# Two expert layers in groups of four and pairs of two, with twelve row fetches ahead and scatters and fetches by turns

## What is computed

```python
# first block, expert capacity 308
probs = softmax(x @ Wr + br); gates, ids = top_k(probs, 2)
h   = silu(einsum('ecd,edh->ech', xg, W1) + b1[:, None, :])     # xg: rows gathered by expert
out = einsum('ech,ehd->ecd', h, W2) + b2[:, None, :]
y   = zeros((N, D)).at[disp_tok].add(out * disp_g)              # scattered back by token

# second block
top_w, top_i = top_k(softmax(xf @ router_w.T), 2); top_w /= sum(top_w)
h = gelu(einsum('nc,ech->enh', xf, w1), approximate=False)
y = einsum('ne,enc->nc', comb, einsum('enh,ehc->enc', h, w2))
```

## Time and profile before

| | |
|---|---|
| time, median of three runs | 1128.98 us (1125.56 to 1130.19) |
| the profiled execution's own span | 1166.7 us |
| PE busy in it | 1021.1 us, 88% |
| DVE, ACT, POOL busy | 846.9, 796.1, 291.8 us |
| expert layer 0, first fetch to last scatter landed | 202.10 to 333.63 us |
| expert layer 1, likewise | 1034.77 to 1150.61 us |
| POOL's indirect DMAs, fetch and block scatter, median of one | 0.968 and 0.985 us |

### The profile page before, as it was taken

One profiled execution on the slowest core, in us unless ns is written; L12 is line 12 of the kernel. 1 busy time (PEld: TensorE's weight loads), 2 busy tenths in 40 slices (PEclk: granted clock), 3 DMA queues, 4 the chain that ended last, 5 costly groups with the idle time before them and its releaser, 6 DMA issues.

```text
span 1166.7 us, 22431 instructions
## 1 busy us (share of the span) xinstructions
PE 1021.1 (88%) x8264; PEld 490.1 (42%) x8268; DVE 846.9 (73%) x1585; ACT 796.1 (68%) x1174; POOL 291.8 (25%) x296
## 2 busy tenths in 40 slices
PE   9747667777888789999999999999999999977785
PEld 6412224777864322332223223232223332447785
DVE  3599997255334789999999999999999991361123
ACT  3653432445555569999999999999999999332122
POOL 0079871555325410000000000000000000036652
PEclk9969998898899889999999999999999999989898
DMA  3055533644123420011100111001111000066333
GB/s 106 1 188 185 194 108 110 199 123 121 55 89 117 143 72 19 17 35 34 35 22 15 35 35 35 19 18 35 35 34 20 17 4 5 3 193 204 116 94 124
DMA packets 57975, 87.94 MB, mean 75 GB/s; under 512 B 26240, under 2 KB 28664, under 8 KB 57484
## 3 DMA queue, kind: packets, MB, share of 16 engines
q1 hardware_dynamic: 51694, 75.52, 21.0%
q0 software_dynamic: 4544, 9.32, 2.6%
q10 hardware_dynamic: 1630, 1.67, 0.5%
HBM read 73.10 MB, written 12.94 MB: 74 GB/s over the span
## 4 chain that ended last, share of the span: by engine, by line
PE 68%; DVE 10%; issue 9%; DMA 4%; ACT 3%; another core or an unknown queue 2%; POOL 2%; SPq 1%; ACTq 0%; DVEq 0%; POOLq 0%
PE psum L959 24%; PE psum L945 22%; PE psum L1084 6%; PE psum L1070 6%; PE psum L949 2%; DVE ssm_h L1738 2%; PE psum L1053 1%; PE psum L789 1%; DVE tile_max L2018 1%; DMA w1r<-y_dram 1%; POOL h0T L1457 1%; DVE ssm_g L1747 1%; PE psum L769 1%; DVE proj_o L2014 1%
## 5 line engine op out<-in xcount | busy, mean ns | idle before, releaser
L1320 ACT ACTIVATE probs<-psum 128x1024 f32<-128x1024 f32 x512 | 505.5, 1041 | 15.1 <-PE psum L949 4.1
L2018 DVE TENSOR_REDUCE tile_max<-psum 128x1 f32<-128x512 f32 x720 | 456.3, 684 | 27.9 <-PE psum L945 26.4
L959 PE MATMUL psum<-probs,v_head 128*32 128x256 f32 (+1 forms) x3840 | 320.8, 406 | 0.7 <-ACT probs L1320 0.4
L945 PE MATMUL psum<-k_stack,q_stack 62*128 62x512 bf16 x994 | 311.2, 397 | 10.9 <-DMA q_stack<-q_dram 7.4
L949 PE MATMUL psum<-q_stack,k_stack 64*128 64x512 bf16 x1024 | 302.8, 384 | 4.1 <-DMA q_stack<-max_parts 3.7
L945 PEld LDWEIGHTS psum<-k_stack,q_stack 62*128 62x128 bf16 x994 | 92.1, 110 | 245.6 <-DVE tile_max L2018 116.5
L1509 POOL TENSOR_TENSOR max_parts<-row_max,no_shift 128x8 bf16<-128x8 f32 x32 | 6.4, 199 | 537.9 <-DVE row_max L1994 537.9
L959 PEld LDWEIGHTS psum<-probs,v_head 128*32 128x32 f32 x3840 | 75.7, 108 | 154.6 <-issue 102.9
L1084 PE MATMUL psum<-w_held,hid 128*128 (+1 forms) x624 | 92.6, 296 | 25.2 <-ACT hid L1379 11.2
L1070 PE MATMUL psum<-x_cols,w1r 128*128 128x128 f32 (+1 forms) x624 | 92.2, 296 | 10.3 <-issue 7.7
L1084 PEld LDWEIGHTS psum<-w_held,hid 128*128 128x128 f32 x624 | 83.7, 208 | 28.4 <-issue 27.2
(11 more groups left out here) (284 smaller groups left out, 1074.8 us busy)
## 6 DMA issues: line engine op xcount, KB each, us to landing
w1r<-w SPq DMA_DIRECT2D x78, 256.0 KB
ssm_b<-bc_dram SPq DMA_DIRECT2D x32, 512.0 KB, 4.1
k_stack<-k_dram SPq DMA_DIRECT2D x60, 120.0 KB
w_held<-w SPq DMA_DIRECT2D x16, 256.0 KB, 4.4
w1r<-y_dram SPq DMA_DIRECT2D x16, 256.0 KB, 5.2
q_stack<-q_dram SPq DMA_DIRECT2D x30, 96.0 KB
bc_p<-bc_dram SPq DMA_DIRECT2D x5, 512.0 KB, 5.7
xtok_dram<-x_tok SPq DMA_DIRECT2D x8, 256.0 KB, 2.4
```

Source lines behind the costliest of these rows:

```text
L945: mm(bank, queries, k_stack[rows, u, keys:keys + C], start=True, stop=True).then_inc(s1_ps, 1)
L959: i = mm(psum[32 * j:32 * j + VM, 7, lo:hi], v_head[:, u, kt, :], probs[:, kt % 4, j * C + lo:j * C + hi], start=kt == 0, stop=kt == KT - ...
L1320: f(probs[:, kt % 4, hf * HALF:(hf + 1) * HALF], banks(2 * slot, 2), ACT.Exp, scale=SCALE).then_inc(p_ready, 1)
L2018: v.tensor_reduce(top, bank, AX.X, ALU.max).then_inc(s1_read, 1)
```

## The change

Both expert layers are regrouped, and POOL's order is new:

- Fetches go straight into `x_cols`, which holds all 32 blocks; `x_got` and its ring are gone. One semaphore counts the fetches of each turn.
- Turns are made in groups (`TURNS`): blocks 0-1, 2-3, then seven groups of four. A group goes into one PSUM bank, and one instruction scales it into `x_cols`, in place.
- `up` and `down` go by pairs of items (20 "units", the last of one item), with four PSUM banks for `up` and four pairs of `hid`. Gelu takes a pair in one instruction; silu keeps four for each item.
- `rows` go by sets of four items (10 sets) in one copy, into buffers for all 39 items (in the space of `lane_hot`, in `y_sum`, and in a new tile); the ring of 6 is gone, and `put` is one semaphore.
- POOL issues 12 fetches, then for each block its scatter and the fetch of the block 12 further on. A scatter waits for its row set's copy.
- PE's order: turns 0 to 2 and units 0 and 1 up first; then for each unit u the turn that starts three units on (if one does), up(u+2), down(u). The gate spreads stand around the downs of units 1 and 2, the capacity rounds behind units 3 to 10, and `gates_turned` behind the loop.

```diff
+UNITS = [(i, min(i + 2, ITEMS)) for i in range(0, ITEMS, 2)]
+TURNS = [(0, 2), (2, 4)] + [(i, i + 4) for i in range(4, BLOCKS, 4)]
+ROW_SETS = [(i, min(i + 4, ITEMS)) for i in range(0, ITEMS, 4)]
+HID_RING = 4
+GETS_FIRST = 12
+def turned_in(u):
+    return [g for g, (first, _) in enumerate(TURNS) if first // 2 == u]
...
+                def turn(g):
+                    first, end = TURNS[g]
+                    pe.wait_ge(got[g], 16 * (end - first) * (layer + 1))
+                    if layer or g:
+                        pe.wait_ge(cols_ready, layer * NT + g)
+                    for i in range(first, end):
+                        at = (i - first) * 128
+                        j = mm(psum[:, TURN_BANK, at:at + 128], x_cols[:, i, :], mat("ident"), start=True, stop=True)
+                    j.then_inc(turned_ps, 1)
...
                 turn(0)
                 up(0)
                 turn(1)
-                for i in range(ITEMS):
-                    if i + 2 < BLOCKS:
-                        turn(i + 2)
-                    if i + 1 < ITEMS:
-                        up(i + 1)
-                    down(i)
+                up(1)
+                turn(2)
+                for u in range(NU):
+                    for g in turned_in(u + 3):
+                        turn(g)
+                    if u + 2 < NU:
+                        up(u + 2)
+                    if layer == 0 and u in SPREAD_UNITS:
+                        spread_gates(2 * SPREAD_UNITS.index(u))
+                    down(u)
+                    if layer == 0 and u in SPREAD_UNITS:
+                        spread_gates(2 * SPREAD_UNITS.index(u) + 1)
+                    if layer == 0 and 0 <= u - COUNT_LATER < ROUNDS:
+                        count_round(u - COUNT_LATER)
+                if layer == 0:
+                    gates_turned()
...
-                columns(0)
-                columns(1)
+                for g in range(3):
+                    columns(g)
                 act.wait_ge(bias_ready, 1)
+                for u in range(NU):
+                    hidden(0, u)
...
+                    for g in turned_in(u + 3):
+                        columns(g)
+                    if u in SPREAD_UNITS:
+                        for c in range(2):
+                            spread(2 * SPREAD_UNITS.index(u) + c)
+                    if u and u % 2 == 0:
+                        rows(u // 2 - 1)
+                rows(NR - 1)
...
                 def get(i):
-                    n = layer * BLOCKS + i
-                    k = n % XG_RING
-                    if n >= XG_RING:
-                        pool.wait_ge(turned_ps, n - XG_RING + 1 + (TILES if i >= XG_RING and layer else 0))
-                    g.indirect_dma_start(x_got[:, k, :], None, xtok_dram,
-                                         bass.IndirectOffsetOnAxis(get_row[:, i:i + 1], 0)).then_inc(got[k], 16)
+                    g.indirect_dma_start(x_cols[:, i, :], None, xtok_dram,
+                                         bass.IndirectOffsetOnAxis(get_row[:, i:i + 1], 0)).then_inc(got[turn_of(i)], 16)
 
                 def send(i):
-                    pool.wait_ge(o_rows_ready, n + 1)
+                    pool.wait_ge(o_rows_ready, layer * NR + i // 4 + 1)
...
-                for i in range(XG_RING):
+                for i in range(GETS_FIRST):
                     get(i)
                 for i in range(BLOCKS):
                     send(i)
-                    if i + XG_RING < BLOCKS:
-                        get(i + XG_RING)
+                    if i + GETS_FIRST < BLOCKS:
+                        get(i + GETS_FIRST)
```

More of the change, by code:

```diff
@@ L110, with turn_of @@
 FIRST_Q_LOADS = 6
+def turn_of(i):
+    return next(g for g, (first, end) in enumerate(TURNS) if first <= i < end)
+def turned_in(u):
+    return [g for g, (first, _) in enumerate(TURNS) if first // 2 == u]
 def placed(layer):
@@ new lines, in up @@
+                def up(u):
+                    unit = layer * NU + u
+                    if unit >= 2:
+                        pe.wait_ge(hidden_ready, unit - 1)
+                    for i in range(*UNITS[u]):
+                        n = layer * ITEMS + i
+                        k = n % W_RING
+                        if i < BLOCKS:
+                            space = x_cols[:, i, :]
+                        else:
+                            if i == BLOCKS:
+                                pe.wait_ge(place_ready, placed(layer)["second"])
+                            at = pe.value_load(cut_block_i[0:1, i - BLOCKS:i - BLOCKS + 1], min_val=0, max_val=BLOCKS - 1)
+                            space = x_cols[:, bass.ds(at, 1), :].rearrange("p o t -> p (o t)")
+                        pe.wait_ge(w1_in[k], 16 * (n // W_RING + 1))
+                        pe.wait_ge(cols_ready, layer * NT + turn_of(min(i, BLOCKS - 1)) + 1)
+                        for hc in range(HC):
+                            j = mm(psum[:, 2 * (unit % 2) + i % 2, hc * 128:(hc + 1) * 128], w1r[:, k, hc * 128:(hc + 1) * 128], space,
+                                   start=True, stop=True)
+                    j.then_inc(hidden_ps, 1)
@@ L1080, in down @@
[L1080 to L1085, removed]
+                    pe.wait_ge(hidden_ready, unit + 1)
+                    if at == 0 and rows >= 2:
+                        pe.wait_ge(o_rows_ready, rows - 1)
@@ new lines, in down @@
+                    for i in range(*UNITS[u]):
+                        e = pe.value_load(tile_expert_i[0:1, i:i + 1], min_val=0, max_val=NE - 1) if i < BLOCKS else i - BLOCKS + 1
+                        space = psum[:, ROW_BANK + rows % 2, i % 4 * 128:(i % 4 + 1) * 128]
+                        for hc in range(HC):
+                            weights = w2_held[:, bass.ds(e, 1), hc, :].rearrange("p o d -> p (o d)")
+                            j = mm(space, hid[:, unit % HID_RING, i % 2, hc, :], weights, start=hc == 0, stop=hc == HC - 1)
@@ L1098, in count_round @@
                     pe.wait_ge(thr_step, rnd * 5 + 4)
[L1099 removed]
+                    mm(psum[:, GATE_BANK, 0:1], mat("group"), thr_f["keep"][:], start=True, stop=True).then_inc(thr_counted, 1)
                 def gates_turned():
@@ L1344, in attention, with hidden @@
                 store_chunks(act, NH - 1, LAST_BY_ACT)
[L1346 to L1349, removed]
-            def silu_blocks():
[L1353 to L1362, removed]
+            def hidden(layer, u):
+                unit = layer * NU + u
+                act.wait_ge(hidden_ps, unit + 1)
+                if unit >= HID_RING:
+                    act.wait_ge(rows_ps, layer * NR + max((u - HID_RING) // 2 + 1, 0))
@@ new lines, in silu_blocks, with columns, rows @@
+            def silu_blocks():
+                def columns(g):
+                    first, end = TURNS[g]
+                    act.wait_ge(turned_ps, g + 1)
+                    f(x_cols[:, first:end, :].rearrange("p b t -> p (b t)"), psum[:, TURN_BANK, 0:(end - first) * 128], ACT.Identity,
+                      scale=modc(0, CB), bias=modc(0, SB)).then_inc(cols_ready, 1)
+                def rows(r):
+                    first, end = ROW_SETS[r]
+                    act.wait_ge(rows_ps, r + 1)
+                    f(o_rows(first, end), psum[:, ROW_BANK + r % 2, 0:(end - first) * 128],
+                      ACT.Identity).then_inc(o_rows_ready, 1)
@@ L1364, in spread @@
                 def spread(c):
                     act.wait_ge(gates_ps, c + 1)
-                    f(chunk(gates_rep, c), psum[:, 3, :], ACT.Identity).then_inc(gates_step, 1)
-                columns(0)
-                columns(1)
+                    f(chunk(gates_rep, c), psum[:, GATE_BANK, :], ACT.Identity).then_inc(gates_step, 1)
+                for g in range(3):
+                    columns(g)
                 act.wait_ge(bias_ready, 1)
[L1371 to L1379, removed]
-                    j.then_inc(hidden_ready, 1)
[L1381 to L1386, removed]
@@ L1394, in weigh @@
+                rows(NR - 1)
+            def gelu_blocks():
+                for u in range(NU):
+                    unit = NU + u
+                    first, end = UNITS[u]
+                    hidden(1, u)
+                    f(hid[:, unit % HID_RING, 0:end - first].rearrange("p i h s -> p (i h s)"), banks(2 * (unit % 2), end - first),
+                      ACT.Gelu).then_inc(hidden_ready, 1)
             def weigh(layer):
```

137 lines of the change are left out of this document (59 added, 78 removed).

## The result

| | before | after |
|---|---|---|
| time, median | 1128.82 us (1125.56 to 1130.19, 4 runs) | 1251.33 us (1249.07 to 1253.99, 4 runs) |
| ratio | | 1.1088 (1.1063 to 1.1113), +122.5 us |
| profiled execution, span and clock | 1166.7 us, 0.947 | 1251.1 us, 0.914 |
| layer 0, first fetch to last scatter landed | 131.5 us | 169.7 us |
| layer 1, likewise | 115.8 us | 155.9 us |

The changed kernel is 11% slower, and its profiled execution, timed at 1252.91 us, agrees with its other runs. The forecast had the direction, but its 1208 us is 43 us short, and the measured median lies 3.3 us above the top of its range.

What follows compares the result with a forecast made beforehand. It took TensorE to do most of the work, with GpSimd loaded but not setting the pace. Layer changes of +40.6 and +41.1 us sum to 81.7, scaled to +79: 1208 us, range 1180 to 1248.

Steps and rivals of the forecast that it cites:

- The ring: Expert layers: row copy, four scatters and four fetches, landing, PE's work and slow clock; 19.7 us per cycle, five per layer.
- The layers' ends: Expert layers: layer 0 ends at 374.7 against 333.6, layer 1 at 1191.2 against 1150.6 before layer 0's shift.
- The step that failed: Whole kernel: 81.7 us more gives 1248.4 profiled; scaled by 0.968, profile to median, +79 and 1208 us; chance 0.73.
- dearer: Rival: the profile's 37.7 us excess lies in old expert-layer waits that the new waits cover; 1248 us, chance 0.14.
- five: Waits on another core or an unknown queue in the two expert layers, 5.34 to 3.46 us; effect taken as zero.
- the last fetch's landing: Each cycle, between a turn's last fetch and PE's start: 2.0 us taken, from bounds of 1.76 and 2.57.
- the tails: Each expert layer after pair 11: last row sets, block scatters, seven cut scatters and landing; 34.0 us.
- PE's turn, up and down: PE's part of each cycle: 4.45 us at full clock plus 2.4 us for the slow clock after waiting.
- faster: Rival: a turn's eight issues overlap and cost GpSimd one 1.28 us step; cycle 8.6 us, 1091 us, chance 0.04.
- no change: Rival: the cycle costs just what pairs and wide copies give back; chance 0.02.
- cheaper: Rival: little clock loss and quick landing, cycles of 17.0 us, 1182 us but still slower than before; chance 0.07.

Runs made afterwards that it cites:

- two further profiles: The kernel before, unchanged, profiled twice more: executions spanning 1118.8 and 1120.5 us, timed at 1120.63 and 1122.43 us.
- second profile: The kernel before, unchanged, profiled again: the execution spans 1118.8 us, its expert layers take 101.3 and 95.5 us.

## Why the prediction was wrong, step by step

**The ring** was right, link by link. Forecast 19.7 us a cycle, five in a layer; measured 19.7 to 20.4 in layer 1 and 19.3 to 20.2 in layer 0. The eight issues with their gaps took 9.97 us (9.93 forecast). PE waited just where it was said, before the turn for the fetch: in layer 1 five times, some nine us each; in layer 0 once for the first fetch (4.75), then 13.07 and four times 8.6 to 9.5. Within the blocks of eight the issues stood 1.27 to 1.31 us apart. The Trainium skill, DMA: Bandwidth & Descriptors, section Anatomy of one DMA, says that many descriptors go out before the added cost is seen. It speaks of descriptors, and the prediction carried that over to eight DMAs, each with descriptors of its own; in that sense these rows do not agree: between the first and the last start of a turn lie 9.00 us.

**The layers' ends** were right too, as positions. Layer 0 was to end at 374.7 and ended at 374.47, in part by luck: it began 2.7 us later than in the first profile and took 169.7 us where the forecast's positions make it 172.6. Layer 1 was to end, as moved by the first, at 1232.3 (1191.2 + 41.1) and ended at 1235.23. The sum gave 1248.4 us for the profiled execution, which spans 1251.1.

**The step that failed** is the last: "scaled by it the change is +79, and 1208 us is my forecast". It took the 37.7 us by which before's profile exceeds the median off the changed kernel as well, as if it were a share of all stages. The two further profiles show it where the *dearer* rival put it, in the old layers, and the new kernel's profile has none of it. The rival's time, 1248, is 3.3 us from the measured median. Its reason was not quite that: it had the old waits covered by the new ones, but they are missing from the kernel before itself in both further profiles. I gave it 0.14 with the remark "nothing places the excess"; six waits on an unnamed queue within two layers of 247 us, and none in the other 919 us of that chain, did place it.

**The same step once more, in the reading.** That GpSimd "is loaded, yet it doesn't set the pace" was read from that profile's 43.9 us of idle time; in the second profile it is 14.0, and 10.4 in layer 1, and GpSimd is the chain for some 40 us of layer 1. The 11.2 us of PE's wait for `hid` from the same rows are 0.3 there. The forecast's "+40.6" (layer 1) and "+41.1" (layer 0) are +40.1 and +38.1 against the first profile, but +60.4 and +68.4 against the second. And the waits were six, not "five".

**Terms that were mis-sized**, all small and of both signs: the last fetch's landing was 2.0 from its issue's end, measured 1.6 to 1.7 (2.52 to 2.67 from its start, less about 1.0); a scatter's 2.24 runs from its issue's start, and I counted it from the end, so the tails measured 32.8 and 32.9 us instead of 34.0; PE's turn, up and down took 7.1 to 7.7 us in the four cycles of layer 1 behind which another wait follows, instead of 6.85. A tail's end in layer 1 of after, where the last scatter starts at 1232.99 and has landed 2.24 later:

```profile
1232.99 2.24 DMA y_dram<-last_rows,cut_row_i
```

The other rivals fell: *faster* and *no change* by the pitch, *cheaper* (17.0) by the clock, which was lost after every wait.

## What to carry to other kernels

When a queue that runs in order interleaves producers and consumers, write down the ring it closes and how far ahead the first lot reaches: here four items more of lead were worth 100 us, and the length of the ring, not any engine's load, set the time. Before a difference is taken against a profile, compare that profile's own time with the timed runs, and if they disagree look for the stage that holds the excess; build the new time up from positions, and don't scale. What a stalled TensorE loses is its wait and then the slow clock behind it. And follow the chain even where a number comes out: with sets of two the cycle was the expected one, over other links.

## What the runs showed of the hardware

An indirect DMA of 128 rows of 512 bytes keeps GpSimd 0.94 to 1.00 us in steady flow, and issues follow each other every 1.24 to 1.31 us, whatever the lead; 71 of them are 90.9 us of GpSimd in a layer of 95.5 to 96.9 us. One execution of a kernel can hold some 28 us of waits of 3.5 to 5.7 us that no record explains, and more behind them by the clock (0.88 and 0.93 granted in the two layers, which were 50.5 us longer together), while two further profiles held none. After some nine us of standing TensorE came back at the lower of its two clock levels, 1.2 GHz: the stretch of turn and up from 1155.50 has a granted clock of 0.50, and there the turn of four took 2.08 us (1.06 with 32 fetches ahead) and an up of two items 3.41 (1.79 in the tail).
